# Products that nobody reads behind each projection of the spiking stage

## The chip, the core and the metric

The kernel runs on one core of a Trainium2 chip. A core has a matrix engine (TensorE, PE in the profile, with its weight loads as PEld), three engines that work on rows (VectorE or DVE, ScalarE or ACT, GpSimd or POOL), a queue that issues transfers (SyncE or SP) and 16 DMA engines. Each engine works through its own list of instructions in order, and the engines wait for one another through semaphores. The metric is the device time of one execution in microseconds (us); lower is better. Three runs of the kernel before took 1256.29, 1257.32 and 1259.03 us, so their median is 1257.32.

## The reference

The input is 8 images of 32 x 64 tokens with 128 channels in fp32. Four blocks are added to it one after the other: a spectral convolution on the sphere, a block that reads opcodes out of a normalised row, a spiking attention, and a mixture of 8 experts of which each token takes two. The change lies in the spiking attention (the 8 images are its time steps):

```python
def lif(x, v_th):
    def step(v, xt):
        v = v + (xt - v) / TAU
        s = heaviside(v - v_th)
        v = v * (1.0 - s)
        return (v, s)
...
def branch(i):
    y = jnp.einsum('tbnc,dc->tbnd', x, lin_w[i]) + lin_b[i]
    y = bn(y, bn_g[i], bn_b[i], bn_m[i], bn_v[i])
    s = lif(y, 1.0)
...
attn = jnp.einsum('tbhnd,tbhmd->tbhnm', q, k) * SCALE
o = jnp.einsum('tbhnm,tbhmd->tbhnd', attn, v)
o = lif(o, 0.5)
y = jnp.einsum('tbnc,dc->tbnd', o, lin_w[3]) + lin_b[3]
return lif(y, 1.0)
```

A neuron's voltage at one time step depends on whether it fired at the step before, so the 8 time steps of one group of tokens have to be worked through one after the other.

## The kernel before

The program runs the spectral convolution, then the synthesis of its output, then `opcode_and_spikes` (the opcode block, the spiking attention and the routing of tokens to experts, all pipelined), and last `experts`. Tokens lie as tiles of 128 rows.

The spiking stage is a loop of 9 iterations `i` (0 to 8; `NP2` is 8) of 8 steps `b` (time steps, 0 to 7). In a step the engines do these things in this order:

- PE: `attend` (L1120) and `project_out` (L1135) for iteration i-1, `project` (L1091) for iteration i, then `key_values` (L1108) in steps 1, 3, 5 and 7, then what stands in `beside` (L1603): in step 0 `route_rank` (from iteration 3) and in steps 0, 1 and 2 a `turn` (four transposes, L1156), in steps 4 and 5 two `route_turn`s (L1170, from iteration 2), in step 6 `route_logits` (L1176, from iteration 2), in step 7 a `turn` for the next iteration.
- ACT: `sign_attended`, `sign_output`, `sign_projected` (L1325, the signs of the projections), `spike_output`, then `behind` (L1535): in steps 0, 1 and 2 first `major` (L1295, which copies the transposes out as zT for a projection two steps on) and then normalised rows (L1266, L1276), in steps 3 to 5 rows and copies for the routing (L1304, L1312).
- DVE: `output`, `attended`, `projected` (L1057 resets the voltage of neurons that fired, L1059 keeps the spikes), then `beside` (L1415), whose first work in steps 0, 2, 4 and 6 is `masked` (L1067): two instructions that read both halves of the bank `ps_kv`, which `key_values` filled one step before, and write `kvm`. Statistics, opcode arithmetic and routing follow in the same step.
- POOL adds the output to the rows and scatters rows to the experts' slots.

`projected` in step b waits for the signs of step b, and the projection of step b+1 waits for the reset of step b. `attend` reads `kvm`: in steps 0 and 1 what `masked` wrote in step 6 before, in steps 2 and 3 what it wrote in step 0, and so on; it waits for

```python
pe.wait_ge(s_kvm, w * 4 + b // 2 + 1)
```

where w is i-1. The projections go to the bank `ps_q`, the attended values to `ps_o`, the outputs to `ps_y`. A projection is two halves of four products: an fp32 one of 128 columns, its bias in bf16, an fp32 one of 256 columns, its bias. In the trace an fp32 product of this kind shows as two matmul records.

Of the kernel before, what the change touches and what calls it, by code (L numbers as in the profile page):

```python
# [24 lines left out]
B, H, W, C = 8, 32, 64, 128  # L25
# [23 lines left out]
NP2 = HP // 2  # L49
# [612 lines left out]
def opcode_and_spikes(nc, t, sb, pb, sem, x_sb, ident, minus_half, weights, slots, routing):  # L662


    wqkv, wo, bias, ones, einv, s_einv = weights
# [10 lines left out]
    with ExitStack() as a:  # L676
# [28 lines left out]
        ps_kv = pb("ps_kv", [P, 2, G * C], at=a)  # L705
        ps_o = pb("ps_o", [P, 512], at=a)
        ps_y = pb("ps_y2", [P, 512], at=a)
# [27 lines left out]
        start = sb("start", [P, PAIRS], at=a)  # L735
# [16 lines left out]
        s_ca = sem("c_added")  # L752
# [39 lines left out]
        s_kvm = sem("e_key_values_masked")  # L792
# [19 lines left out]
        def need(eng, s, value):  # L812

            if value > 0:
                eng.wait_ge(s, value)
# [4 lines left out]
        def orders_turned(pe, i, g):  # L820

            need(pe, s_chT, (i - 1) * 2 + g + 1)
            for q in range(G):
                ins = nc.tensor.transpose(ps_kv[:, g, q * P:(q + 1) * P],
                                          h_sb[:, g * G + q, 2 * i:2 * i + 2].rearrange("p h r m -> p (h r m)"), ident[:, :])
            ins.then_inc(s_ct, 1)
# [7 lines left out]
        def grid(pe, i, g):  # L834

            pe.wait_ge(s_chT, i * 2 + g + 1)
            for h in range(2):
                u = (i * 2 + g) * 2 + h
                need(pe, s_ca, u - 1)
                for q in range(2):  # L840
                    at = (h * 2 + q) * P
                    ins = nc.tensor.matmul(grid_bank(u)[:, q * 2 * C:(q + 1) * 2 * C], hT[:, g, at:at + P], einv[:, :],
                                           start=True, stop=True)
                ins.then_inc(s_cg, 1)
# [242 lines left out]
        def add_into(out, lhs, rhs, first):  # L1087

            return nc.tensor.matmul(out, lhs, rhs, start=first, stop=True, skip_group_check=True)  # L1089

        def project(pe, w, b):  # L1091

            k = w * B + b
            if b % 2 == 0:
                pe.wait_ge(s_zT, w * G + b // 2 + 1)
            if b:
                pe.wait_ge(s_rq, w * LAST + b)
            else:
                need(pe, s_sq, k)
            for j in range(2):  # L1100
                q, dst = 2 * b + j, ps_q[:, j]
                add_into(dst[:, 0:P], wqkv[:, 0:C], zT[:, q, :], b == 0)
                add_into(dst[:, 0:P], bias[:, 0:C], ones[:, b, :], False)
                add_into(dst[:, P:3 * P], zT[:, q, :], wqkv[:, C:3 * C], False)
                ins = add_into(dst[:, P:3 * P], ones[:, b, :], bias[:, C:3 * C], False)
            ins.then_inc(s_qkv, 1)

        def key_values(pe, w, bp):  # L1108

            pe.wait_ge(s_spk, w * B + 2 * bp + 2)  # L1110
            need(pe, s_kvm, w * 4 + bp)
            for n in range(4):
                b, j = 2 * bp + n // 2, n % 2
                for ip in range(2):
                    rows = slice(64 * ip, 64 * ip + 64)
                    ins = nc.tensor.matmul(ps_kv[:, ip, n * C:(n + 1) * C], spk[rows, b, j, C:2 * C],
                                           spk[rows, b, j, 2 * C:3 * C], start=True, stop=True)
            ins.then_inc(s_kv, 1)

        def attend(pe, w, b):  # L1120

            pe.wait_ge(s_kvm, w * 4 + b // 2 + 1)
            if b:
                pe.wait_ge(s_ro, w * LAST + b)
            else:
                need(pe, s_sgo, w * B)
            for j in range(2):
                for ip in range(2):
                    n = (b % 2) * 2 + j
                    ins = add_into(ps_o[:, j * P + ip * 64:j * P + ip * 64 + 64],  # L1130
                                   kvm[:, (b // 2) % 2, ip, n * C:(n + 1) * C],
                                   spk[:, b, j, ip * 64:ip * 64 + 64], b + j + ip == 0)
            ins.then_inc(s_o, 1)
# [15 lines left out]
        def turn(pe, w, g):  # L1149

            pe.wait_ge(s_z, w * G + g + 1)
            need(pe, s_zT, w * G + g)
            if g == 0:
                need(pe, s_rz, (w - 3) * G + 3)
            for q in range(G):
                ins = nc.tensor.transpose(ps_t[:, 0, q * P:(q + 1) * P], z[:, g * G + q, :], ident[:, :])  # L1156
            ins.then_inc(s_tr, 1)

        def route_turn(pe, v, g):

            pe.wait_ge(s_ry, v * G + g + 1)
            if g == 0:
                pe.wait_ge(s_zT, min(v + 3, NP2) * G)
                need(pe, s_rz, v * G - 1)
            elif g == 1:
                need(pe, s_ranked, v)
            else:
                pe.wait_ge(s_rz, v * G + g - 1)
            for q in range(G):
                ins = nc.tensor.transpose(ps_t[:, g % 2, q * P:(q + 1) * P], r_y[:, g * G + q, :], ident[:, :])  # L1170
            ins.then_inc(s_rt, 1)

        def route_logits(pe, v):
            pe.wait_ge(s_rz, v * G + 4)
            for q in range(NT):
                ins = nc.tensor.matmul(ps_log[:, q * E:(q + 1) * E], rT[:, q, :], wg[:, :], start=True, stop=True)  # L1176
            ins.then_inc(s_lg, 1)

        def route_rank(pe, v):

            pe.wait_ge(s_ch, v + 1)
            nc.tensor.matmul(ps_rank, before[:, :], chosen[:, :, :].rearrange("p q e -> p (q e)"), start=True, stop=False)
            for d in range(1, NT + 1):
                ins = nc.tensor.matmul(ps_rank[:, d * PAIRS:], every[:, :],
                                       chosen[:, 0:NT + 1 - d, :].rearrange("p q e -> p (q e)"), start=False, stop=(d == NT))
            ins.then_inc(s_rk, 1)
# [162 lines left out]
        with nc.Block() as block:  # L1349
# [242 lines left out]
            @block.tensor  # L1592
            def _(pe):
                pe.wait_ge(s_einv, 16)
                for i in range(NP2):
                    for g in range(2):
                        orders_turned(pe, i, g)
                    for g in range(2):
                        grid(pe, i, g)
                pe.wait_ge(s_set, 1)  # L1600
                turn(pe, 0, 0)

                def beside(i, b):  # L1603

                    n, r = i + 1, i - 2
                    if b == 0 and r >= 1:
                        route_rank(pe, r - 1)
                    if b in (0, 1, 2) and i < NP2:
                        turn(pe, i, b + 1)
                    if b in (4, 5) and r >= 0:  # L1610
                        route_turn(pe, r, 2 * b - 8)
                        route_turn(pe, r, 2 * b - 7)
                    if b == 6 and r >= 0:
                        route_logits(pe, r)
                    if b == LAST and n < NP2:
                        turn(pe, n, 0)

                for i in range(NP2 + 1):
                    for b in range(B):
                        k = (i - 1) * B + b  # L1620
                        if k == 0:
                            pe.wait_ge(s_ca, 4 * NP2)
                        if k >= 0:
                            attend(pe, i - 1, b)
                        if k >= 1:
                            project_out(pe, *divmod(k - 1, B))
                        if i < NP2:
                            project(pe, i, b)
                        if b in (1, 3) and i:
                            key_values(pe, i - 1, b // 2 + 2)  # L1630
                        if b in (5, 7) and i < NP2:
                            key_values(pe, i, b // 2 - 2)
                        beside(i, b)
                project_out(pe, NP2 - 1, LAST)
                route_rank(pe, NP2 - 2)
                for g in range(G):
                    route_turn(pe, NP2 - 1, g)
                route_logits(pe, NP2 - 1)
                route_rank(pe, NP2 - 1)
# [348 lines left out]
```

## Time and profile before

| | |
|---|---|
| median of three runs | 1257.32 us |
| the profiled execution | 1256.02 us, span 1254.1 us |
| PE busy | 982.3 us (78%) |
| DVE busy | 827.8 us (66%) |
| ACT busy | 626.2 us (50%) |
| POOL busy | 565.3 us (45%) |
| mean granted TensorE clock | 0.864 of full speed |

The span is cut into 40 slices of 31.4 us each on the profile's page. The eighth of them ends at 250.8 us, where the first projection of the spiking stage starts, and the last projection ends at about 671 us; the experts run from about 796 us on. A digit is a share of busy time in tenths, and PEclk is the clock that TensorE was granted, in tenths of full speed:

```profile
PE   9958848766668677767776541399999999999997
...
DVE  7724435755869889798865472166666666666665
ACT  3434414476596877877762430144444444444443
...
PEclk9979969977787888787886555699999999999999
```

In the stage no engine is busy all the time, and the clock lies between its two levels, 1.2 and 2.4 GHz (granted clock 0.50 and 1.00), on average. In the experts PE is busy throughout at the full clock.

### The profile page before, as it was taken

What the parts mean: (1) busy time and instruction counts of PE and PEld (TensorE: products, weight loads), DVE (VectorE), ACT (ScalarE), POOL (GpSimd) and SP (SyncE); (2) the same over time, 40 slices, a digit from 0 to 9 for tenths busy, and PEclk for the clock granted to TensorE, in tenths of its full rate; (3) what the DMA queues carried; (4) which work ended last, traced back from release to release, by engine and by line L of the source; (5) the groups of instructions that cost most, each with busy time, mean ns of one, the idle gap of its engine ahead of it and who ended that gap; (6) DMA issues with size and microseconds to landing.
All of it is one profiled execution on the core that took longest, in us unless ns stands there. A gap on an engine that the chain in (4) does not pass through costs nothing. (4 is left out here: it accounts for less than half of the span.)

```text
span 1254.1 us, 23605 instructions
## 1 busy us (share of the span) xinstructions
PE 982.3 (78%) x6627; PEld 824.6 (66%) x6628; DVE 827.8 (66%) x2676; ACT 626.2 (50%) x1334; POOL 565.3 (45%) x730
## 2 busy tenths in 40 slices
PE   9958848766668677767776541399999999999997
PEld 7848826544456465555555530288888888888886
DVE  7724435755869889798865472166666666666665
ACT  3434414476596877877762430144444444444443
POOL 3310001112223667675664777355545554555454
PEclk9979969977787888787886555699999999999999
DMA  9569587900010110000000000111111111111110
GB/s 371 253 185 292 179 229 179 214 19 20 20 51 20 35 38 25 12 29 14 33 16 21 30 25 34 46 41 42 45 48 43 47 50 50 46 42 49 49 40 2
DMA packets 83330, 93.56 MB, mean 75 GB/s; under 512 B 7708, under 2 KB 75548, under 8 KB 79929
## 3 DMA queue, kind: packets, MB, share of 16 engines
q1 hardware_dynamic: 74201, 75.33, 20.3%
q0 software_dynamic: 9056, 17.33, 4.2%
q8 instruction: 37, 0.61, 0.2%
q14 instruction: 36, 0.29, 0.1%
HBM read 56.07 MB, written 38.32 MB: 75 GB/s over the span
## 5 line engine op out<-in xcount | busy, mean ns | idle before, releaser
L1738 POOL DMA_INDIRECT out_dram<-res,index x155 | 154.8, 999 | 215.7 <-DVE res L1804 187.8
L1847 ACT ACTIVATE sil<-ps_h 128x512 f32<-128x512 f32 x155 | 92.6, 597 | 253.0 <-PE ps_h L1899 253.0
L1769 DVE TENSOR_TENSOR act_rows<-ps_h,sil 128x512 f32<-128x512 f32 x155 | 107.3, 692 | 131.8 <-ACT sil L1847 131.8
L1918 PE MATMUL ps_y<-r_raw,aT 128*128 x1240 | 163.8, 275 | 0.0
L1918 PEld LDWEIGHTS ps_y<-r_raw,aT 128*128 128x128 f32 x1240 | 150.7, 192 | 0.1
L159 POOL DMA_INDIRECT slots<-x_sb,r_pos x128 | 131.4, 1027 | 42.1 <-issue 37.1
L1897 PE MATMUL ps_h<-r_raw,uTh 128*128 x310 | 136.5, 440 | 1.8 <-DVE uTl L1763 1.6
L1898 PE MATMUL ps_h<-r_raw,uTh 128*128 x310 | 123.6, 399 | 0.0
L1899 PE MATMUL ps_h<-r_raw,uTl 128*128 x310 | 121.9, 393 | 0.0
L1089 PE MATMUL ps_q<-wqkv,zT 128*128 128x256 f32 x256 | 114.5, 540 | 0.0
L1201 POOL TENSOR_TENSOR x_sb<-x_sb,sy 128x256 f32<-128x256 f32 x64 | 43.0, 672 | 146.5 <-ACT sy L1347 146.4
L1089 PE MATMUL ps_q<-zT,wqkv 128*128 128x128 f32 x256 | 71.6, 372 | 34.5 <-DVE ps_q L1057 18.9
L1907 PE MATMUL ps_a<-ident,act_rows 128*128 128x128 f32 x620 | 92.8, 272 | 0.1
L1853 ACT ACTIVATE aT<-ps_a 128x512 f32<-128x512 f32 x155 | 91.7, 592 | 1.0 <-PE ps_a L1907 1.0
L219 POOL TENSOR_TENSOR e_tmp<-e_tmp,minus_half 128x16 f32<-128x16 f32 x16 | 47.1, 2944 | 99.5 <-DVE e_tmp L203 99.2
L1907 PEld LDWEIGHTS ps_a<-ident,act_rows 128*128 128x128 f32 x620 | 77.0, 140 | 21.4 <-DVE act_rows L1769 0.3
L1325 ACT ACTIVATE sig_q<-ps_q,under_one 128x768 bf16<-128x768 f32 x64 | 57.4, 897 | 65.9 <-PE ps_q L1089 65.8
L1089 PEld LDWEIGHTS ps_q<-zT,wqkv 128*128 128x128 f32 x256 | 53.3, 258 | 55.4 <-ACT zT L1295 20.5
L512 PE MATMUL ps_m<-sblk,wc 128*128 128x128 f32 x512 | 61.7, 286 | 20.8 <-DVE sblk L463 14.1
L1728 POOL TENSOR_SCALAR u_rows<-pay 128x127 f32<-128x127 f32 x156 | 73.3, 478 | 7.7 <-DMA pay<-slots 6.4
L512 PEld LDWEIGHTS ps_m<-sblk,wc 128*128 128x128 f32 x512 | 61.1, 202 | 21.6 <-issue 21.6
L1057 DVE SCALAR_TENSOR_TENSOR ps_q<-sig_q,ps_q 128x768 f32<-128x768 bf16 x56 | 53.6, 956 | 29.7 <-ACT sig_q L1325 29.7
(239 smaller groups left out, 2368.3 us busy)
## 6 DMA issues: line engine op xcount, KB each, us to landing
wc<-in_mixing_weights SPq DMA_DIRECT2D x8, 2048.0 KB, 14.1
slots<-zero SPq DMA_DIRECT2D x4, 2652.0 KB, 23.2
pay<-slots SPq DMA_DIRECT2D x39, 272.0 KB, 2.8
x_sb<-in_token_rows SPq DMA_DIRECT2D x8, 1088.0 KB, 5.7
sblk<-coefficients SPq DMA_DIRECT2D x16, 256.0 KB, 5.9
mixed<-mo SPq DMA_DIRECT2D x16, 256.0 KB, 7.5
gin<-mixed SPq DMA_DIRECT2D x16, 256.0 KB, 14.2
r_raw<-in_L_ffn_W SPq DMA_DIRECT2D x8, 508.0 KB
```

The source lines that it names most:

```text
L159: nc.gpsimd.indirect_dma_start(slots, bass.IndirectOffsetOnAxis(at, 0), x_sb[:, tile, :], None).then_inc(self.s_sc, 16)
L512: ins = nc.tensor.matmul(ps_m[:, half, t, :], wc[:, n % WS, l, m, :], sblk[:, n % SB, :, l, 4 * m:4 * m + 4].rearrange("p h m f -> p h (m ...
L1089: return nc.tensor.matmul(out, lhs, rhs, start=first, stop=True, skip_group_check=True)
L1738: nc.gpsimd.indirect_dma_start(out_rows, bass.IndirectOffsetOnAxis(at, 0), res[:, m % RES, :], None, bounds_check=TOKENS - 1, oob_is_err=F ...
L1769: nc.vector.tensor_tensor(act_rows[:, k], ps_h[:, k, :, DFF:], sil[:, k], ALU.mult).then_inc(s_act, 1)
L1847: nc.scalar.activation(sil[:, k], ps_h[:, k, :, 0:DFF], ACT.Silu).then_inc(s_sil, 1)
L1853: nc.scalar.activation(aT[:, k, :], ps_a[:, :], ACT.Copy).then_inc(s_ac, 1)
L1897: nc.tensor.matmul(dst, hi, upper_w[:, :, col], start=True, stop=False)
L1898: nc.tensor.matmul(dst, hi, lower_w[:, :, col], start=False, stop=False)
L1899: ins = nc.tensor.matmul(dst, lo, upper_w[:, :, col], start=False, stop=True)
L1907: ins = nc.tensor.transpose(ps_a[:, h * P:(h + 1) * P], act_rows[:, k, h // 2, (h % 2) * P:(h % 2 + 1) * P], ident[:, :])
L1918: ins = nc.tensor.matmul(dst, aT[:, k, (2 * e + h) * P:(2 * e + h + 1) * P], raw[:, 4 + h, col], start=(h == 0), stop=(h == 1))
```

## The change

A function `keep_busy` is added to PE's program and called right behind each `project`, ahead of `key_values` and `beside`. It issues products of the identity with a constant table (`einv`, fp32, 256 columns) whose results are never read. In iteration 0 there are two behind each projection, into the banks `ps_o` and `ps_y`, which hold nothing yet (ahead of the first, PE waits until the rows of the earlier stage are out of these banks). In iterations 1 to 7 there is one, into the first half of the bank `ps_kv`, and ahead of it PE waits on the semaphore `s_kvm`, which `masked` raises.

```diff
+        def keep_busy(pe, w, b):
+
+            def idle_product(bank):
+                nc.tensor.matmul(bank[:, 0:2 * C], ident[:, :], einv[:, :], start=True, stop=True)
+
+            if w == 0:
+                if b == 0:
+                    pe.wait_ge(s_ca, 4 * NP2)
+                idle_product(ps_o)
+                idle_product(ps_y)
+            else:
+                pe.wait_ge(s_kvm, w * 4 + b // 2 - 2)
+                idle_product(ps_kv[:, 0])
+
         def key_values(pe, w, bp):
...
                         if i < NP2:
                             project(pe, i, b)
+                        if i < NP2:
+                            keep_busy(pe, i, b)
                         if b in (1, 3) and i:
                             key_values(pe, i - 1, b // 2 + 2)
```

The change adds 14 lines ahead of L1108, so lines of `kernel.py` behind it have other numbers after (L1116 is L1130, L1156 is L1170, L1176 is L1190); the new product is L1111. PE's list in iteration 4 around step 2, from the last product of the projection on, is this before (the brackets name the semaphores that a row waits on):

```order
L1089 MATMUL ps_q<-bias,ones 128x256
L1156 MATMUL ps_turn<-ident,z 128x128 [waits e_channel_major,e_normalised]
L1156 MATMUL ps_turn<-ident,z 128x128 x3
L1089 MATMUL ps_o<-spk,kvm 128x64 [waits e_attended_reset,e_key_values_masked]
L1089 MATMUL ps_o<-spk,kvm 128x64 x3
```

And at the same place in the changed kernel:

```order
L1089 MATMUL ps_q<-bias,ones 128x256
L1111 MATMUL ps_kv<-einv,ident 128x256 [waits e_key_values_masked]
L1170 MATMUL ps_turn<-ident,z 128x128 [waits e_channel_major,e_normalised]
L1170 MATMUL ps_turn<-ident,z 128x128 x3
L1089 MATMUL ps_o<-spk,kvm 128x64 [waits e_attended_reset,e_key_values_masked]
```

The transposes of the turn, and all that follows them, now stand behind a product that waits for `masked`. In step 6 of the same iteration PE's list before holds the logits of the routing right behind the projection:

```order
L1089 MATMUL ps_q<-bias,ones 128x256
L1176 MATMUL ps_turn<-wg,rT 128x8 [waits r_channel_major]
L1176 MATMUL ps_turn<-wg,rT 128x8 x15
L1089 MATMUL ps_o<-spk,kvm 128x64 [waits e_attended_reset,e_key_values_masked]
L1089 MATMUL ps_o<-spk,kvm 128x64 x3
```

And in the changed kernel:

```order
L1089 MATMUL ps_q<-bias,ones 128x256
L1111 MATMUL ps_kv<-einv,ident 128x256 [waits e_key_values_masked]
L1190 MATMUL ps_turn<-wg,rT 128x8 [waits r_channel_major]
L1190 MATMUL ps_turn<-wg,rT 128x8 x15
L1089 MATMUL ps_o<-spk,kvm 128x64 [waits e_attended_reset,e_key_values_masked]
```

Here the logits stand behind the new wait. The lists of DVE, ACT, POOL and SP are the same in both kernels.

## Rows read from the trace of the kernel before

**Rows 1.** Busy time, granted clock by iteration; columns: PE, PEld, DVE, ACT, POOL, PEclk, DMA, GB/s

```profile
297.08:347.71 50.63, 34.34 (x240) 25.36 (x240) 33.59 (x123) 34.30 (x83) 11.46 (x13) 0.77 0.08 20
...
564.67:620.17 55.50, 39.10 (x305) 29.57 (x305) 44.97 (x163) 42.90 (x106) 34.33 (x43) 0.85 0.06 21
```

**Rows 2.** What the projections' bank made others wait for (us, times)

```profile
  DVE ps_q L1057: 32.0, 40
...
  ACT sig_q L1325: 65.8, 33
```

**Rows 3.** One projection at either clock: PE busy (x), PEclk, DMA, GB/s

```profile
454.51:456.60 2.09, 2.01 (x12) 1.00 0.16 50
504.08:507.80 3.72, 3.70 (x12) 0.52 0.06 19
```

**Rows 4.** Timeline, iteration 4, step 2: start, us, engine, line, op, names, shapes, idle before

```profile
472.41 0.58 ACT L1295 ACTIVATE zT<-ps_turn 128x512 f32<-128x512 f32 x1
...
473.46 1.28 DVE L1067 SCALAR_TENSOR_TENSOR kvm<-ps_kv,mask 128x512 bf16<-128x512 f32 x2
...
473.72 0.65 PE L1089 MATMUL ps_q<-wqkv,zT 128*128 128x256 f32 x2
...
474.21 0.27 PE L1089 MATMUL ps_q<-bias,ones 128*128 128x256 bf16 x1
...
477.06 0.90 ACT L1325 ACTIVATE sig_q<-ps_q,under_one 128x768 bf16<-128x768 f32 x1
...
479.02 0.95 DVE L1057 SCALAR_TENSOR_TENSOR ps_q<-sig_q,ps_q 128x768 f32<-128x768 bf16 x1
...
479.08 0.28 PE L1089 MATMUL ps_o<-spk,kvm 128*128 128x64 bf16 x4 [3.39 <-DVE ps_o L1076]
```

**Rows 5.** Timeline, iteration 4, step 0

```profile
458.42 0.38 PE L1182 MATMUL ps_turn<-chosen,before 128*128 128x476 bf16 x1 [1.89 <-DVE chosen L981]
...
460.27 0.64 PE L1156 MATMUL ps_turn<-ident,z 128*128 128x128 f32 x4
460.43 1.28 DVE L1067 SCALAR_TENSOR_TENSOR kvm<-ps_kv,mask 128x512 bf16<-128x512 f32 x2
...
460.94 0.60 ACT L1295 ACTIVATE zT<-ps_turn 128x512 f32<-128x512 f32 x1 [3.14 <-PE ps_turn L1156]
```

**Rows 6.** Timeline, iteration 4, step 4

```profile
486.52 0.66 PE L1170 MATMUL ps_turn<-ident,r_y 128*128 128x128 f32 x4 [2.31 <-ACT r_y L1304]
...
486.90 1.27 DVE L1067 SCALAR_TENSOR_TENSOR kvm<-ps_kv,mask 128x512 bf16<-128x512 f32 x2
...
487.01 0.30 PE L1089 MATMUL ps_o<-spk,kvm 128*128 128x64 bf16 x4
...
487.96 0.74 PE L1089 MATMUL ps_q<-zT,wqkv 128*128 128x128 f32 x2
...
491.23 0.90 ACT L1325 ACTIVATE sig_q<-ps_q,under_one 128x768 bf16<-128x768 f32 x1 [1.54 <-PE ps_q L1089]
```

**Rows 7.** Timeline, iteration 4, step 6

```profile
500.76 1.28 DVE L1067 SCALAR_TENSOR_TENSOR kvm<-ps_kv,mask 128x512 bf16<-128x512 f32 x2
...
507.82 0.90 ACT L1325 ACTIVATE sig_q<-ps_q,under_one 128x768 bf16<-128x768 f32 x1 [2.19 <-PE ps_q L1089]
```

**Rows 8.** Timeline, iteration 3: the logits products at the full clock

```profile
442.59 3.64 PE L1176 MATMUL ps_turn<-wg,rT 128*128 128x8 f32 x32
```

**Rows 9.** Timeline of PE after the stage, clock at half: rank and logits products

```profile
679.85 3.38 PE L1184 MATMUL ps_turn<-chosen,every 128*128 128x448 bf16 x16
...
708.47 6.94 PE L1176 MATMUL ps_turn<-wg,rT 128*128 128x8 f32 x32
```

**Rows 10.** The 4 us behind idle PE stretches of 3.4 us (three of six)

```profile
297.08:301.08 4.00, 4.00 (x14) 3.14 (x15) 0.56 (x2) 2.02 (x6) 0.00 (x0) 0.50 0.07 19
...
479.08:483.08 4.00, 3.69 (x23) 2.88 (x24) 4.00 (x14) 2.61 (x7) 3.17 (x3) 0.65 0.11 35
...
591.26:595.26 4.00, 3.70 (x25) 2.82 (x26) 3.90 (x12) 2.60 (x7) 3.18 (x3) 0.71 0.10 35
```

## The prediction

> **What bounds the kernel now.** I read the 40 slices first: from 796 us on PE is busy throughout at the full clock, and the change adds nothing there. It adds work between 251 and 671 us, so I read the table of that stretch by iteration: PE is busy 34 to 39 of some 51 to 56 us, its granted clock is 0.77 to 0.85 on average [rows 1], and no engine is the limit by its busy time. Then the waits at the bank of the projections: ACT waited 65.8 us in 33 places for a projection to end, PE waited 32.0 us in 40 for the reset of the voltages [rows 2]. The stage is a ring: projection, signs on ACT, reset on DVE, next projection, and at some steps ACT's own row work is later than the projection. Last I read timelines of one iteration, the fourth, engine by engine, at the places where the new products stand. A projection takes 2.01 us at the full clock and 3.70 at half [rows 3]; where ACT waits for it, half clock costs 1.7 us.
>
> **What is added: 72 products.** 16 in iteration 0 and 8 in each of seven iterations. The same form, 256 fp32 columns, holds PE from 473.72 to 474.21, 0.49 us at the full clock [rows 4], so I take 0.98 at half. Laid end to end that is 35 to 71 us of PE, but PE waits behind most projections (the 40 places above).
>
> **What the wait costs: the main term.** The semaphore counts the masks. Before step 0 of iteration w it stands at 4w-3, and the product of step 0 waits for 4w-2; steps 2, 4 and 6 each want one more. The mask that raises it comes on DVE in that same step, behind signs, reset and spikes of the very projection that the new product follows. So in steps 0, 2, 4 and 6 of iterations 1 to 7, 28 times, PE now stops behind a projection until its mask has ended, and the whole queue behind stops with it: turn, rank or logits, attended values, output and next projection. Before, `attend` asked for that mask two steps later. In odd steps the value has been reached already and there is no wait. I walk iteration 4, at the full clock; the brackets give the place of the times.
>
> - Step 2 [rows 4]: the mask ends at 473.46 + 1.28 = 474.74. Product 0.49, then the turn, 0.64 [rows 5]: the transposes end at 475.87. ACT copies them to zT right behind the signs of step 2; it did so at 472.41, now 3.46 later, and behind it, without a pause, come nine rows and the signs of the next step (477.06). DVE gives some back: those signs ended at 477.96, but the next reset began at 479.02, so DVE had 1.06 of other work. Net 2.4 us.
> - Step 0 [rows 5]: the mask ends at 461.71. Product 0.49, rank 1.85 (458.42 to 460.27), turn 0.64: 464.69. zT, for which ACT already waited 3.14, began at 460.94. Net 3.75.
> - Step 4 [rows 6]: the mask ends at 488.17. Product 0.49, two sets of transposes 1.32, attended values and output 0.95 (487.01 to 487.96), projection 2.01: 492.94. The signs of step 5 waited for the projection and began at 491.23. Net 1.7.
> - Step 6: the mask ends at 502.04 [rows 7]. Product 0.49, logits 3.64 [rows 8], 0.95, 2.01: 509.13, against 507.82 [rows 7]. Net 1.3; more where the old projection of step 7 ran at the full clock.
>
> At the full clock that is 9.15 us an iteration. With everything at half, each PE piece twice as long, projection 3.70 and logits 6.94 [rows 9]: step 0 6.7 (rank 3.38 for its long part, rows 9), step 2 3.5, step 4 6.2, step 6 7.7, together 24.2.
>
> Which of the two? The wait leaves PE idle for signs, reset, spikes and mask, 0.9 + 0.95 + 0.35 + 1.28 = 3.5 us at the least (0.35 is my estimate for the spikes, the rest from rows 4). Stretches of 3.4 us are in the trace (one ends at 479.08, rows 4): in the 4 us behind them the clock was 0.50, 0.65 and 0.71, mean 0.62 [rows 10]. So the first 4 us behind each mask do 2.48 us of full-clock work. Step 2 has 1.13 us of it on its path, 0.7 longer, net 3.1. Steps 0 and 4 have more than 2.48, each 1.52 longer: 5.3 and 3.2. Step 6 too, and the projection behind the long logits ran near half clock before (504.08, clock 0.52, rows 3), another 1.7: 4.5. Together 16.1 us an iteration.
>
> Iterations 3 to 7 are alike: 5 x 16.1 = 80.5. Iteration 2 has no rank but the rest; its turn stood right behind the projection, so the loss is about the same, 16. Iteration 1 has no logits and no routing transposes either: 8.4 for steps 0 and 2, and I take 2.6 for the others, 11. Sum 107.5.
>
> **What the clock gives back.** Were the clock full in the whole stage, the 33 waits of ACT would each lose the half-clock part of a projection: 33 x 1.7 x 0.38 = 21 us (0.38 is twice what is missing to 1 at a mean clock of 0.81, between the ends of rows 1). That is the upper end; the lower is 0. I take 6: the added columns stand in the even steps behind the idle stretch, not in it, and at several steps DVE would be late anyway, as the 1.06 shows.
> The Trainium skill ("TensorE: Matmul & The Clock Gate", "What's actually happening") says that the slow clock is the default and that activity releases it. By that rule alone the products would raise the clock, and the sum would have the 21 in place of the 6. The trace agrees that idle stretches are followed by half clock (0.50 to 0.71 above), and this change makes 28 longer ones.
>
> **What costs nothing.** The two products of iteration 0 (0.98 us, 1.96 at half) and their wait: they stand while signs and reset, 1.85 us, run before PE may go on. Bounds: below, -5 (a few projections at full clock there); above, +8, for eight times about 1 us if the turns behind them hold ACT. The 28 products of odd steps likewise stand in PE's wait for the reset; at half clock without that cover, 28 x 0.98 = 27 us. I take 0 for both.
>
> **Sum.** 107.5 - 6 = 102 us (rounded) on the profiled execution's 1256.0 us gives 1358. That execution is 1.3 us below the median of the three runs, which is nothing against these terms, so I predict 1358 us.
>
> **Rivals.**
>
> - *Waits at the full clock* (12%). The products and the shifted work keep PE awake, all 28 waits cost their full-clock price and all of 21 us comes back: 7 x 9.15 - 21 = +43, 1299 us. For it: bursts behind the masks are dense. Against: the idle stretch comes first, each time.
> - *Half clock throughout* (12%). The stretches are so long that the clock hardly recovers: 7 x 24.2 = +169, 1425 us. For it: mask end lies 3.5 us or more behind every even projection. Against: the bursts of 5 us behind them, and that DVE and ACT would then hide part of PE's slowness.
> - *The wait is no wait* (3%). The count is reached before PE comes to it, so the change does what its words say: spare products in PE's idle time, and the 21 us come back: 1235 us, faster. It decides if `masked` of a step ends before that step's projection does. Against: DVE's list holds the mask behind the reset, and the reset waits for the signs of that projection; only a mistake of mine in counting would do it.
> - *Nothing moves* (2%): loss and gain cancel, 1257 us. It would take a gain of over 60 us from the clock, three times the 21.
>
> **How the numbers follow.** The forecast has 71%. Its own range, from taking step 6 and step 0 nearer either clock, is 1320 to 1395. The range for 8 in 10 is 1295 to 1405: it takes in the full-clock rival, and the half-clock one in part, since odd steps or the first iteration could add their bounds without all of it being at half. A change of 0.2% (2.5 us) is about what a measurement here can tell from none. Slower has 71 + 12 + 12 = 95%, same 2%, faster 3%.
>
> **What would show it.** In the profile after: L1111 waits for DVE's `kvm` in the even steps, some 1 to 4 us each beyond what PE waited there before; ACT's wait for the turn's transposes grows by 3 us in steps 0 and 2; iterations 2 to 7 last 65 to 75 us in place of 51 to 56, and all stages behind are shifted but unchanged. The mean clock from 297 us to the end of the stage stays near 0.8 or falls. I am wrong if that clock rises above 0.9, or if L1111 in even steps begins within a microsecond of its projection's end.

## The result, and the profile after

The changed kernel takes 1378.79 us (median of 4 runs, 1375.33 to 1379.54) against 1256.8 for the kernel before (4 runs beside them, 1255.31 to 1259.03): 1.098 times as long, interval 1.0947 to 1.1008, or 122 us more. The forecast was 1358 us, with 1295 to 1405 as its range. The profiled execution after has a span of 1373.4 us, 119.3 more than before.

The 40 slices of the page after (34.3 us each), for the engines shown of before:

```profile
PE   9958578665557666767666744319999999999997
...
DVE  7644436465564757565667375506666666666675
ACT  3435234645664646564663443104444444444443
...
PEclk9989789878987777777778755559999999999999
```

The dip of PEclk to 5, behind the spiking stage, starts in slice 23 of before (from 22 x 31.4 = 691 us) and in slice 24 here (from 23 x 34.3 = 789 us), and the experts behind it look the same. Ahead of it the digits of DVE and ACT are lower: the same work with more idle time. The waits of the whole execution, largest first (engine, line, waited for: us in total, times, longest), say who idles:

```profile
PE ps_kv L1111 <- DVE kvm L1067: 129.6, 28, 6.4
...
ACT zT L1309 <- PE ps_turn L1170: 83.9, 16, 8.9
...
ACT sig_q L1339 <- PE ps_q L1089: 52.8, 30, 3.6
```

The new product waits 129.6 us for `masked` in 28 places, 4.6 us each. Not all of this is new idleness: the wait of the attended products for their reset (`ps_o` L1089 on L1076), 59.7 us in 28 places before, is 26.2 in 15 here. ACT now waits 83.9 us in 16 places for the transposes, where it had waited 13.8 in 6, and 52.8 for projections, where it had waited 65.8 [rows 2]. By iteration, with the columns of [rows 1] (iterations 1, 4 and 6 stand here):

```profile
299.55:361.60 62.05, 37.40 (x257) 28.18 (x257) 33.67 (x123) 34.37 (x83) 11.37 (x13) 0.78 0.13 36
...
504.57:579.66 75.09, 50.53 (x321) 39.77 (x321) 48.52 (x187) 43.22 (x106) 37.04 (x45) 0.75 0.05 16
...
654.59:727.50 72.91, 49.01 (x321) 38.74 (x322) 44.49 (x161) 43.22 (x106) 33.54 (x42) 0.77 0.05 16
```

Iteration 1 went from 50.63 to 62.05 us and iteration 6 from 55.50 to 72.91, its clock from 0.85 to 0.77 [rows 1]. From the first projection of iteration 1 to the last of iteration 7 it was, before:

```profile
297.08:671.30 374.22, 274.41 (x2033) 212.91 (x2035) 293.68 (x1100) 275.19 (x665) 198.56 (x239) 0.81 0.09 26
```

and after:

```profile
299.55:791.05 491.50, 326.17 (x2140) 257.47 (x2141) 295.24 (x1100) 276.49 (x664) 196.67 (x239) 0.77 0.07 20
```

This is +117.3 us of the 119.3. DVE and ACT have the same busy time as before, so they work as much and wait longer. PE has 52 us more of busy time, at a lower clock, and 65.5 us more of idle time (99.8 before, 165.3 after).

The timeline of iteration 4, step 2, beside [rows 4] (start, us, engine, line, operation, names, shapes, idle before):

```profile
527.05 0.89 ACT L1339 ACTIVATE sig_q<-ps_q,under_one 128x768 bf16<-128x768 f32 x1
...
529.20 1.28 DVE L1067 SCALAR_TENSOR_TENSOR kvm<-ps_kv,mask 128x512 bf16<-128x512 f32 x2
...
530.53 1.22 PE L1111 MATMUL ps_kv<-einv,ident 128*128 128x256 f32 x2 [3.97 <-DVE kvm L1067]
...
531.54 1.06 PE L1170 MATMUL ps_turn<-ident,z 128*128 128x128 f32 x4
...
532.64 0.60 ACT L1309 ACTIVATE zT<-ps_turn 128x512 f32<-128x512 f32 x1 [4.39 <-PE ps_turn L1170]
...
533.13 3.56 ACT L1290 ACTIVATE x_sb<-x_sb,e_tmp 128x128 f32<-128x128 f32 x9
...
537.31 0.89 ACT L1339 ACTIVATE sig_q<-ps_q,under_one 128x768 bf16<-128x768 f32 x1
```

The mask ends at 530.48, and PE starts 0.05 us later, after 3.97 us of idleness. zT begins 2.16 us behind the mask's end, where before it began 2.33 us ahead of it; nine rows follow it on ACT, and then the signs of the next step. Step 0, beside [rows 5]:

```profile
510.34 1.27 DVE L1067 SCALAR_TENSOR_TENSOR kvm<-ps_kv,mask 128x512 bf16<-128x512 f32 x2
...
511.67 1.22 PE L1111 MATMUL ps_kv<-einv,ident 128*128 128x256 f32 x2 [5.08 <-DVE kvm L1067]
...
513.08 3.09 PE L1198 MATMUL ps_turn<-chosen,every 128*128 128x448 bf16 x16
...
516.01 0.63 PE L1170 MATMUL ps_turn<-ident,z 128*128 128x128 f32 x4
...
516.68 0.60 ACT L1309 ACTIVATE zT<-ps_turn 128x512 f32<-128x512 f32 x1 [8.82 <-PE ps_turn L1170]
```

Here the rank stands between the mask and the turn, and ACT waits 8.82 us for the transposes, where it had waited 3.14. Step 6, beside [rows 7]:

```profile
562.57 1.27 DVE L1067 SCALAR_TENSOR_TENSOR kvm<-ps_kv,mask 128x512 bf16<-128x512 f32 x2
...
563.90 1.22 PE L1111 MATMUL ps_kv<-einv,ident 128*128 128x256 f32 x2 [3.78 <-DVE kvm L1067]
...
564.92 6.83 PE L1190 MATMUL ps_turn<-wg,rT 128*128 128x8 f32 x32
...
576.39 0.90 ACT L1339 ACTIVATE sig_q<-ps_q,under_one 128x768 bf16<-128x768 f32 x1 [3.05 <-PE ps_q L1089]
```

The logits take 6.83 us, as at half clock [rows 9], and the signs of step 7 come 12.55 us behind the mask's end, where before it was 5.78 [rows 7]. The stretches from a mask's end to what ACT waits for, in step 6, 0, 2 and 4 (the sixth number behind the length is PEclk):

```profile
563.84:576.39 12.55, 12.49 (x59) 11.45 (x60) 3.28 (x20) 4.13 (x11) 5.81 (x8) 0.50 0.03 7
511.61:516.68 5.07, 5.01 (x29) 3.24 (x30) 0.48 (x5) 0.00 (x0) 0.00 (x0) 0.60 0.02 3
530.48:532.64 2.16, 2.11 (x11) 1.76 (x12) 1.95 (x5) 0.00 (x0) 2.16 (x1) 0.50 0.00 0
547.54:554.30 6.76, 6.71 (x35) 5.77 (x36) 4.00 (x21) 3.33 (x8) 0.96 (x1) 0.58 0.06 21
```

In step 6 the clock is at its lower level from the mask to the signs. In steps 0 and 4 it rises within the stretch.

### The profile page after: what moved, and what is told of

Same layout as the page of the kernel before. It is cut to its first block and busy times, and to the rows that moved or that the text cites. A ratio compares the mean times of both kernels' runs of the same rounds, so it can differ in the third digit from the quotient of the medians.

```text
span 1373.4 us, 23893 instructions
## 1 busy us (share of the span) xinstructions
PE 1040.5 (76%) x6771; PEld 874.6 (64%) x6772; DVE 829.6 (60%) x2676; ACT 627.5 (46%) x1334; POOL 562.8 (41%) x730
## 5 line engine op out<-in xcount | busy, mean ns | idle before, releaser
L1215 POOL TENSOR_TENSOR x_sb<-x_sb,sy 128x256 f32<-128x256 f32 x64 | 43.0, 671 | 271.2 <-ACT sy L1361 270.9
L1111 PE MATMUL ps_kv<-einv,ident 128*128 128x256 f32 x112 | 51.7, 556 | 129.6 <-DVE kvm L1067 129.6
L1111 PEld LDWEIGHTS ps_kv<-einv,ident 128*128 128x128 f32 x112 | 23.4, 260 | 145.2 <-DVE kvm L1067 140.8
L1085 DVE SCALAR_TENSOR_TENSOR ps_y<-sig_y,ps_y 128x256 f32<-128x256 bf16 x56 | 24.0, 428 | 139.5 <-ACT sig_y L1354 139.1
L1089 PE MATMUL ps_q<-wqkv,zT 128*128 128x256 f32 x256 | 103.0, 490 | 0.0
L1923 PEld LDWEIGHTS ps_a<-ident,act_rows 128*128 128x128 f32 x620 | 77.1, 140 | 21.5 <-DVE act_rows L1785 0.3
L1089 PE MATMUL ps_q<-zT,wqkv 128*128 128x128 f32 x256 | 66.9, 351 | 24.6 <-DVE ps_q L1057 13.6
L1339 ACT ACTIVATE sig_q<-ps_q,under_one 128x768 bf16<-128x768 f32 x64 | 57.3, 895 | 52.8 <-PE ps_q L1089 52.8
L1089 PEld LDWEIGHTS ps_q<-zT,wqkv 128*128 128x128 f32 x256 | 50.2, 244 | 42.2 <-ACT zT L1309 15.7
## 6 DMA issues: line engine op xcount, KB each, us to landing
slots<-zero SPq DMA_DIRECT2D x4, 2652.0 KB, 23.6
```

Of the source, the lines that this page charges most:

```text
L1111: nc.tensor.matmul(bank[:, 0:2 * C], ident[:, :], einv[:, :], start=True, stop=True)
L1923: ins = nc.tensor.transpose(ps_a[:, h * P:(h + 1) * P], act_rows[:, k, h // 2, (h % 2) * P:(h % 2 + 1) * P], ident[:, :])
```

## Where the time went, step by step

The table is worked out from the starts of all the signs of projections on ACT (`sig_q`): the time from one to the next, summed over iterations 1 to 7, less the same of the kernel before. Column "behind 0" goes from the signs of step 0 to those of step 1. The other kernels are those of the experiments below.

| us, one profile each | behind 0 | 1 | 2 | 3 | 4 | 5 | 6 | 7 | sum |
|---|---|---|---|---|---|---|---|---|---|
| changed kernel | 37.7 | -1.0 | 30.6 | -11.0 | 30.3 | -6.2 | 45.4 | -7.4 | 118.3 |
| wait only | 35.0 | -1.0 | 23.7 | -11.0 | 24.6 | -4.7 | 37.3 | -7.4 | 96.5 |
| odd steps only | 2.8 | -1.0 | 0.0 | -1.2 | -0.3 | -3.9 | 0.0 | -4.3 | -7.9 |
| odd steps and step 6 | 1.9 | -0.6 | -0.1 | -0.8 | 0.9 | -5.2 | 49.0 | -7.4 | 37.7 |
| behind `beside` | 8.9 | -0.5 | 23.6 | -10.9 | 22.6 | -6.2 | 2.5 | -7.4 | 32.6 |
| the same, wait only | 7.7 | -0.5 | 15.3 | -10.9 | 18.0 | -6.2 | -3.3 | -7.5 | 12.5 |
| earlier wait | 10.5 | -1.0 | 8.1 | -5.5 | 2.9 | -6.2 | 18.3 | -5.8 | 21.3 |
| mask ahead | 26.5 | -1.0 | 20.0 | -11.0 | 19.3 | -6.2 | 28.2 | -7.4 | 68.3 |

The table leaves out what comes ahead of iteration 1: the first projection of the stage starts between 250.7 and 257.5 us in these profiles, though nothing ahead of it was changed. A profiled execution can also lie some way from the median of its kernel (mask ahead: 1323.32 against 1331.16 us). Where PE waits for the mask behind a projection (behind the signs of steps 0, 2, 4 and 6) time is lost; behind the odd steps part of it comes back.

## The experiments

The theory: PE's list stands still behind 28 waits for `masked`, and what stands behind them then runs at a low clock. Rivals: the products themselves cost the time, or the odd steps or the first iteration do. Each diff is against the changed kernel; ratios are against runs of the kernel before on the same chip (medians 1253.96 to 1255.16 us).

**The wait without the product.** In iterations 1 to 7 PE waits and issues nothing.

```diff
                 pe.wait_ge(s_kvm, w * 4 + b // 2 - 2)
-                idle_product(ps_kv[:, 0])
```

> In iterations 1 to 7 the wait on the mask stays and the product behind it is left out (iteration 0 keeps its pairs). Theory (the queue behind the wait is what costs): most of the loss stays, 1335 to 1385 us, and the losses fall in the steps behind steps 0, 2, 4 and 6. Rival A (PE's own time for the products, 51.7 us busy in the profile, is what costs): near the kernel before, 1255 to 1275 us. Rival B (half clock behind long idle is the larger part): also 1335 us or more, but with step lengths behind a mask that shrink wherever the clock is full.

Measured: 1353.94 us, 1.0783 (1.0739 to 1.0827). Its stretch from the first projection of iteration 1 to the last of 7:

```profile
300.27:770.97 470.70, 295.51 (x2033) 236.58 (x2035) 295.42 (x1100) 276.65 (x665) 196.79 (x239) 0.77 0.07 21
```

And its step 2 of iteration 4:

```profile
518.32 1.28 DVE L1067 SCALAR_TENSOR_TENSOR kvm<-ps_kv,mask 128x512 bf16<-128x512 f32 x2
...
519.66 1.12 PE L1169 MATMUL ps_turn<-ident,z 128*128 128x128 f32 x4 [3.70 <-DVE kvm L1067]
...
520.81 0.60 ACT L1308 ACTIVATE zT<-ps_turn 128x512 f32<-128x512 f32 x1 [3.44 <-PE ps_turn L1169]
```

Lines behind L1120 have numbers lower by one in this kernel. The turn waits for the mask without a product ahead of it. So the wait alone brings about 98 of the 122 us. The granted clock is 0.77 with and without the 56 products: beside the 28 waits they raise nothing. They cost some 22 us more (the table's sums), 21 of it behind steps 2, 4 and 6, about 1 us each, which is the product at half clock.

**Products in the odd steps only.** The first iteration stays as it is.

```diff
-                        if i < NP2:
+                        if i < NP2 and (i == 0 or b % 2):
                             keep_busy(pe, i, b)
```

> The products of iterations 1 to 7 stay in the odd steps alone, where their wait is already met; the 28 of the even steps and their waits are left out. Theory: no new wait, so the 122 us are gone, and even projections at full clock may give back some: 1235 to 1262 us. Rival A (the products' own time): half of the products, so about a half of the loss, 1300 to 1330 us. Rival B (clock): 1225 to 1255 us if the odd products alone keep the clock up.

Measured: 1250.36 us (10 runs), 0.9957 (0.9931 to 0.9984). Its iterations 1 to 7:

```profile
304.60:670.80 366.20, 270.90 (x2084) 211.58 (x2085) 294.77 (x1100) 274.10 (x664) 198.41 (x239) 0.86 0.09 27
```

The 28 products of the odd steps cost nothing, and the interval lies a little below 1. No other version's median is lower, though the intervals of the nearest ones overlap with this one. Here, with no wait added, the clock of the stage is 0.86 against 0.81. Over whole executions it was 0.879 to 0.892 in its 10 runs and 0.861 to 0.870 in the 13 of the kernel before beside them.

**The first iteration only.**

```diff
-                        if i < NP2:
+                        if i == 0:
                             keep_busy(pe, i, b)
```

> Only the pairs of iteration 0 stay; the products and waits of iterations 1 to 7 are left out. Theory: the pairs stand in PE's wait for the reset and cost or bring at most a microsecond or two: 1251 to 1259 us, same as before. Rival: if they hold ACT's copies of the transposes, up to 8 us slower, 1262 us; if the clock is what they bring, 5 us faster, 1250 us.

Measured: 1255.17 us, 1.0008 (0.9983 to 1.0033). The pairs and their wait cost nothing that can be measured.

**Step 6 too.** Odd steps and step 6 have the product and its wait; steps 0, 2 and 4 have neither.

```diff
-                        if i < NP2:
+                        if i < NP2 and (i == 0 or b % 2 or b == 6):
                             keep_busy(pe, i, b)
```

> As the kernel with products in odd steps alone (1250 us), with the wait on the mask and its product added in step 6 of iterations 1 to 7 only, ahead of the logits. Theory: the step behind it, which grew by 45 us over seven iterations in the changed kernel, grows by about as much, and the next step 0 gives back some 5 to 10: 1280 to 1292 us. Rival (the steps' losses hang together through the clock, a share of each would vanish alone): 1262 to 1278 us.

Measured: 1295.97 us, 1.0332 (1.0293 to 1.0371), 46 more than with the odd steps alone, and above what was expected. Its waits:

```profile
PE ps_kv L1111 <- DVE kvm L1067: 32.7, 7, 5.5
```

Seven waits of 4.7 us cost 46 us, 6.5 each. The table puts 49.0 behind step 6. A wait in this place costs more than PE waits in it, since the logits behind it then run at half clock: 6.83 us in each of the six iterations that have them, against 3.64 to 4.42 with the odd steps alone.

**The wait and product behind `beside`.** In even steps of iterations 1 to 7 `keep_busy` is called after turn, rank and logits, so only the attended values, the output and the next projection stand behind it.

```diff
-                        if i < NP2:
+                        if i < NP2 and (i == 0 or b % 2):
                             keep_busy(pe, i, b)
...
+                        if 0 < i < NP2 and b % 2 == 0:
+                            keep_busy(pe, i, b)
```

> In the even steps of iterations 1 to 7 the wait and its product move behind the turn, the rank, the routing transposes and the logits of that step; all 72 products stay. Theory: what stood behind the wait was the cost, so steps 0, 2 and 6 lose little (there the row work or the logits run beside the wait), step 4 still 1 to 3 us an iteration: 1255 to 1300 us. Rival A (the products' own time) and rival B (the clock behind idle stretches): as after, 1360 to 1390 us.

Measured: 1290.95 us, 1.0270 (1.0227 to 1.0312). Behind steps 0 and 6, where rank and logits stand ahead of the wait now, the loss falls from 37.7 to 8.9 and from 45.4 to 2.5. Behind steps 2 and 4 most of it stays, 23.6 and 22.6: `attend` and the next projection still stand behind the mask, as in all even steps, and neither rank nor logits fill the time ahead of it. In step 2 of iteration 4 PE still waited 4.83 us. That step 2 would be free was wrong.

**The same without the 28 products**, the wait kept.

```diff
                         if 0 < i < NP2 and b % 2 == 0:
-                            keep_busy(pe, i, b)
+                            pe.wait_ge(s_kvm, i * 4 + b // 2 - 2)
```

> As the kernel whose wait and product in even steps stand behind the turn, rank, routing transposes and logits (1291 us), with those 28 products left out and the 28 waits kept; odd steps as there. Theory: the wait still holds the attended values and the next projection in steps 2 and 4, and the product adds to that, so between: 1258 to 1278 us. Rival A (the products alone made the 36 us there): 1246 to 1257 us. Rival B (the wait alone): 1284 to 1295 us.

Measured: 1269.43 us, 1.0111 (1.0071 to 1.0151), 19 more than with the odd steps alone; the products are the other 21.5. Its waits (the wait is put down to `attend` here):

```profile
PE ps_o L1089 <- DVE kvm L1067: 66.0, 25, 5.8
```

PE waits 66.0 us in these places and the kernel loses 19. Most of the 66.0 replaces a wait that was there without them. This is what the attended products wait for otherwise, with the odd steps alone and then here:

```profile
PE ps_o L1089 <- DVE ps_o L1076: 54.8, 26, 4.3
...
PE ps_o L1089 <- DVE ps_o L1076: 13.9, 7, 4.3
```

From the first projection of iteration 1 to the signs of the last, this kernel and then the one with step 6 too show:

```profile
299.75:686.32 386.57, 267.62 (x2084) 210.14 (x2085) 296.08 (x1100) 275.59 (x664) 196.70 (x239) 0.86 0.09 26
...
297.44:709.30 411.86, 292.06 (x2098) 232.64 (x2099) 293.46 (x1100) 275.61 (x665) 198.01 (x239) 0.81 0.08 24
```

PE is idle for 119.0 us here and for 119.8 with step 6 too, against 95.3 with the odd steps alone: 24 us are added in both. Here PE's busy time doesn't grow (267.6, against 270.9), and the loss is about what was added. With step 6 too the busy time grows by 21 us, and the loss is 46. So the length of a wait is not its price: what it adds to the idleness that was there, and what the work behind it then takes, is.

**An earlier wait.** In even steps the product goes into the unused half of `ps_o` and waits for the reset of the attended values, which DVE does ahead of the mask.

```diff
-                pe.wait_ge(s_kvm, w * 4 + b // 2 - 2)
-                idle_product(ps_kv[:, 0])
+                if b % 2:
+                    pe.wait_ge(s_kvm, w * 4 + b // 2 - 2)
+                    idle_product(ps_kv[:, 0])
+                else:
+                    pe.wait_ge(s_ro, (w - 1) * LAST + b + 1)
+                    idle_product(ps_o[:, 2 * P:4 * P])
```

> In the even steps of iterations 1 to 7 the product goes into the unused half of the bank of the attended values and waits for the reset of these, which DVE does ahead of the reset of the projections, some 2.5 to 3.3 us before the mask has ended. Place and number of products are those of the changed kernel. Theory: the loss follows the length of the wait: 1250 to 1300 us. Rival A (the products' own time): 1360 to 1390 us. Rival B (clock behind idle stretches): the stretches shrink to some 1.5 us, so 1235 to 1265 us and a clock above 0.9 in the stage.

Measured: 1277.28 us, 1.0151 (1.0097 to 1.0204). Who waited for what was written to `ps_o`:

```profile
  PE ps_o L1111: 48.6, 24
```

The same 72 products, with 48.6 us of waits in place of 129.6, cost 23 us in place of 122. PE's idle time in iterations 1 to 7 is 98.4 us, as before the change (99.8), so here it is PE's longer busy time that shows (297.1 us, 274.4 before).

**The product right ahead of `attend`.** In even steps it waits for what `attend` waits for next anyway.

```diff
-                        if i < NP2:
+                        if i < NP2 and (i == 0 or b % 2):
                             keep_busy(pe, i, b)
...
+                        if 0 < i < NP2 and b % 2 == 0:
+                            pe.wait_ge(s_ro, (i - 1) * LAST + b + 1)
+                            nc.tensor.matmul(ps_o[:, 2 * P:4 * P], ident[:, :], einv[:, :], start=True, stop=True)
```

> The odd steps as in the kernel with products in odd steps alone. In the even steps of iterations 1 to 7 the product stands right ahead of the attended products of the next step, in the unused half of their bank, and waits for the reset that these wait for anyway, so no wait is added and nothing but that step's own chain is held. Theory (only added waits and what they hold cost): 1243 to 1256 us, same or a little faster than before. Rival A (a product in an even step costs its PE time in the ring, as between the wait alone and the changed kernel, 18 to 25 us): 1268 to 1280 us. Rival B (more columns keep the clock up): 1230 to 1245 us.

Measured: 1252.8 us, 0.9981 (0.9957 to 1.0005). All 72 products with no wait before rank, turn or logits cost nothing.

**Two products in each odd step.**

```diff
                 idle_product(ps_kv[:, 0])
+                idle_product(ps_kv[:, 1])
...
-                        if i < NP2:
+                        if i < NP2 and (i == 0 or b % 2):
                             keep_busy(pe, i, b)
```

> As the kernel with products in odd steps alone, but with two products in each odd step, one into each half of the bank of the key-value products. Theory: they still stand in PE's wait for the reset in steps 1 and 3, and hold transposes for 0.5 us more in steps 1, 5 and 7: 1246 to 1258 us. Rival A (PE's time in the ring): 28 x 0.5 to 1 us more than with one, 1264 to 1280 us. Rival B (clock): 1235 to 1246 us with a clock above 0.92 in the stage.

Measured: 1251.31 us, 0.9973 (0.9946 to 1.0001): not to be told from one product. The clock over its runs was 0.884 to 0.898, the highest of all, and bought no more.

**The mask ahead.** DVE's list has `masked` ahead of `projected` in even steps, so it no longer waits for reset and spikes.

```diff
-                    if b in (0, 2, 4) and i:
-                        masked(dve, i - 1, b // 2 + 1)
-                    if b == 6 and i < NP2:
-                        masked(dve, i, 0)
...
+                        if b in (0, 2, 4) and i:
+                            masked(dve, i - 1, b // 2 + 1)
+                        if b == 6 and i < NP2:
+                            masked(dve, i, 0)
```

> All 72 products and the waits stay as in the changed kernel; on DVE the mask of steps 0, 2, 4 and 6 moves ahead of the reset and the spikes of that step, so that the value that PE waits for is reached earlier, while the reset comes 1.28 us later where DVE did not wait there. Theory: PE's stop shrinks from 3.5 us or more to 1 us or less, and what remains is the product and at most 28 x 1.28 us on the reset: 1260 to 1300 us. Rival A (the products' own time): 1365 us or more. Rival B (clock): 1245 to 1275 us with the clock behind the masks back at 0.7 or more.

Measured: 1331.16 us, 1.0624 (1.0567 to 1.0681). This expectation was missed. PE still waited 28 times:

```profile
  PE ps_kv L1111: 91.3, 28
```

That is 3.3 us each, where 1 us or less was expected. Step 4 of iteration 4 shows why:

```profile
514.40 0.27 PE L1089 MATMUL ps_q<-bias,ones 128*128 128x256 bf16 x1
...
515.13 0.90 ACT L1339 ACTIVATE sig_q<-ps_q,under_one 128x768 bf16<-128x768 f32 x1
...
517.51 0.43 DVE L1085 SCALAR_TENSOR_TENSOR ps_y<-sig_y,ps_y 128x256 f32<-128x256 bf16 x1
...
518.32 1.28 DVE L1067 SCALAR_TENSOR_TENSOR kvm<-ps_kv,mask 128x512 bf16<-128x512 f32 x2
...
519.65 1.22 PE L1111 MATMUL ps_kv<-einv,ident 128*128 128x256 f32 x2 [4.98 <-DVE kvm L1067]
```

DVE begins the step's first work only 2.38 us behind the start of the signs, since the opcode arithmetic of the step before is still running. The mask then ends at 519.60, 4.9 us behind the projection. In this step the mask was held by DVE's list, more than by the reset.

A product with no wait at all in the even steps was not tried. The versions without even products and the one ahead of `attend` stand in its place. Nor was a version run whose waits stay while the clock behind them is full, so how the 98 us of the waits divide between standing still and the low clock is worked out from timelines alone.

## Why the prediction was right, and where it was off

*The waits are real, 28 of them, and they are the main term.* Right. L1111 begins within 0.06 us of each mask's end in the timelines above, and the wait alone brings 98 of 122 us. The rivals "the wait is no wait" and "nothing moves" fall with it. PE's wait is 4.6 us on average. The 1 to 4 that the forecast named were meant beyond what PE waited there before, and PE's idle time in iterations 1 to 7 grew by 65.5 us, 2.3 for each of the 28. The rivals "waits at the full clock" (+43) and "half clock throughout" (+169) lie on either side of what was measured.

*The terms of the steps.* With the 2.6 us of iteration 1 halved between steps 4 and 6, the forecast was 7 x 5.3 = 37.1 behind step 0, 7 x 3.1 = 21.7 behind step 2, 20.5 behind step 4 and 28.3 behind step 6. The table has 37.7, 30.6, 30.3 and 45.4. From step 2's the forecast had netted 7 x 1.06 = 7.4 for DVE's other work, which belongs to the column behind 3, so its own loss was forecast as 29.1. Steps 0 and 2 were right in size. In step 0 some luck is in it: DVE began the resets there 4.1 us later in sum than before (3.2 us behind the ends of the signs before, 7.3 after), which the forecast did not have.

*Step 6 is the term that was mis-sized*: 17 us more. The forecast let the first 4 us behind the mask run at clock 0.62, the rest at full, and one projection near half: 7.09 + 1.52 + 1.7 = 10.3 us from the mask's end to the signs of step 7. It was 12.55, all at 0.50, and 12.41 to 12.54 in the other five iterations with logits. That is 2.2 us too little each, 13 of the 17. The walk adds some 5: before the change, the signs of step 7 came 5.78 us behind the mask's end in iteration 4, but 4.31 to 5.62 in the other five, so more was lost there than iteration 4 shows. For this step the rival "half clock throughout" (7.7 us an iteration) was nearer than the forecast (4.5): iteration 4 lost 7.1. The run with odd steps and step 6 confirms the size, 46 us.

*Step 4* lost 10 us more than forecast. In iteration 4 its reset comes 3.19 us behind its signs (541.80 to 544.99), before it was 1.96 (483.73 to 485.69). Before and after:

```profile
483.73 0.90 ACT L1325 ACTIVATE sig_q<-ps_q,under_one 128x768 bf16<-128x768 f32 x1 [2.03 <-PE ps_q L1089]
...
485.69 0.95 DVE L1057 SCALAR_TENSOR_TENSOR ps_q<-sig_q,ps_q 128x768 f32<-128x768 bf16 x1
...
541.80 0.90 ACT L1339 ACTIVATE sig_q<-ps_q,under_one 128x768 bf16<-128x768 f32 x1
...
544.99 0.96 DVE L1057 SCALAR_TENSOR_TENSOR ps_q<-sig_q,ps_q 128x768 f32<-128x768 bf16 x1
...
547.59 1.22 PE L1111 MATMUL ps_kv<-einv,ident 128*128 128x256 f32 x2 [6.26 <-DVE kvm L1067]
```

The signs of step 4 come sooner behind those of step 3 than before (4.49 us against 6.66), DVE isn't ready for them, and 1.2 us of what was given back behind step 3 is lost here. Over the seven iterations these resets begin 5.4 us later behind the signs than before; the other 4 to 5 us are lost behind the mask.

*What the clock gives back* was taken as 6, with 21 as its upper end. The columns behind odd steps sum to -25.6. Part of this is DVE, whose other work no longer holds up the resets. In step 3 that brought 5.2 us (they began 5.5 us in sum behind the ends of the signs before, 0.3 after) in place of the 7.4 netted for it; in steps 1 and 5 up to 6.2 more (7.0 before, 0.8 after), which the forecast did not have. So 14 to 20 us are left for the clock, near the upper end. They don't come from the products: with the wait alone the same columns sum to -24.1. Of the 28 projections in even steps 23 ran at the full clock (under 2.1 us) where before 10 did, and 22 with the wait alone. After the waits PE's work comes in one piece; that this is the reason is not shown. So the losses were 29 us larger than forecast (17 in step 6, 10 in step 4) and the gains 12 larger than the 6 and 7.4 together: 118.3 in place of the forecast's 101.5, which is the 17 us by which the profiled execution (1375.33 us) lies above 1358. That the two errors have opposite signs, so that the total came out closer than its terms, is luck.

*The clock behind the masks.* 0.62 was taken from stretches of 3.4 us [rows 10]. In the 4 us behind all 28 masks after it was 0.54 on average, and 0.50 behind each of iteration 4's. PE had waited 3.45 to 6.44 us there, in all but three places over 3.5 us. With the mask ahead, where the waits were 3.3 us on average, it was 0.63. That the longer waits are the reason is likely by this, but not shown. The 0.65 and 0.71 of those rows are half clock for a part of the stretch only.

*Odd steps and iteration 0 at nothing.* Right: 0.9957 and 1.0008 by themselves. One row behind it was misread: the 32.0 us in 40 places [rows 2] are waits of PE's products (18.9 us in 26) and of its weight loads (13.1 in 14) taken together, so the products waited for the reset in 26 places. The busy time of PE by iteration was 34 to 43 us, not 34 to 39. Neither changes the sum.

The Trainium skill ("TensorE: Matmul & The Clock Gate", "What's actually happening") has the slow clock as the default that activity releases. The runs agree where products are added without a wait (0.81 before, 0.86 with those of the odd steps, in iterations 1 to 7), and show where it doesn't help: with the 28 waits the clock was 0.77 with and without products, and with the waits behind `beside` 0.83 with the 28 products of the even steps and 0.86 without them.

## What to carry to other kernels

Before putting filler into an engine's idle time, find which instruction raises the semaphore it waits on, and how long after the filler's place: an in-order queue carries that wait to everything behind it. Price such a wait by the idleness that it adds to what the engine had anyway, and by what stands behind it and who waits for that, all of it at the lower clock until the trace shows the clock rising, rather than by its length: seven waits of 4.7 us cost 46 us here, while 25 of 2.6 us, most of which replaced older waits, cost 19. Filler paid here only where it added no wait, and that was 0.4% at best.

## What the runs showed of the hardware

Behind a wait of 3.78 us PE was busy for 12.49 of 12.55 us, with logits products for more than half of that, and its granted clock was 0.50 throughout; behind one of 5.08 us, with the rank products, it was 0.60 over 5.07 us. A clock that is higher need not buy time: 0.884 to 0.898 with two products in odd steps and 0.879 to 0.892 with one gave the same time within the intervals.
